# A hand-written schedule of an opening, ordered anew across five engines

## What is computed

```python
x = x + tanh(g_xattn) * matmul(fake_quant(layernorm(x)), fake_quant(ctx))      # 8-bit codes, round and clip 0..255
A, g = quant_act(layernorm(x))       # blocks of 16 to fp8; the last 128 columns twice
gate = A @ quant_w(w_gate).T * g     # weights: blocks of 16 to int4, 2752 x 1024
up   = A @ quant_w(w_up).T * g
h    = silu(gate) * up
x    = x + tanh(g_ffn) * (quant_act(h) @ quant_w(w_down).T) * gm
```

## Time and profile before

| | |
|---|---|
| three runs, median | 793.53 us (793.03 to 793.79) |
| the profiled execution | 792.68 us, span 790.6 us |
| PE busy | 729.5 us, 92% of the span |
| DVE busy | 537.0 us, 68% |
| POOL busy | 339.9 us, 43% |
| ACT busy | 304.2 us, 38% |

### The profile page before, as it was taken

The page is one execution under the profiler, slowest core; times in us unless marked ns, Lnnn a source line. Parts: engine busy times, 40 slices in busy tenths (PEclk is TensorE's granted clock), DMA queues, the critical chain, the costliest instruction groups (busy, mean ns, idle before and its releaser), DMA issues.

```text
span 790.6 us, 10396 instructions
## 1 busy us (share of the span) xinstructions
PE 729.5 (92%) x3472; PEld 333.5 (42%) x3472; DVE 537.0 (68%) x966; ACT 304.2 (38%) x394; POOL 339.9 (43%) x207
## 2 busy tenths in 40 slices
PE   3578249999999999999999999999999999999998
PEld 0233124554444444444444444444444444444443
DVE  2588888952757565665758575747988888988700
ACT  5699965441434334342524252422222312231300
POOL 4435997791857657474847574730000000000000
PEclk9998659999999999999999999999999999999999
DMA  7933696376697969798888889854456474545410
GB/s 291 408 126 109 184 199 133 90 157 155 133 231 161 208 163 223 173 200 204 183 195 182 211 192 213 181 132 160 94 144 208 122 192 115 149 130 124 107 45 27
DMA packets 228885, 131.56 MB, mean 166 GB/s; under 512 B 201713, under 2 KB 212977, under 8 KB 227825
## 3 DMA queue, kind: packets, MB, share of 16 engines
q1 hardware_dynamic: 228848, 131.12, 67.4%
HBM read 61.88 MB, written 19.66 MB: 103 GB/s over the span
## 4 chain that ended last, share of the span: by engine, by line
PE 86%; POOL 3%; DMA 3%; SPq 3%; ACT 2%; issue 2%; DVE 1%; ACTq 0%
PE acc L1373 55%; PE acc L1440 28%; DMA big<-in_ctx_dram 2%; PE acc L1315 2%; DMA mid<-big 1%; POOL h_in L765 1%; SPq L477 1%; SPq L359 1%; ACT big L928 1%; POOL big L742 0%; POOL wbuf_all L735 0%; POOL big L748 0%; POOL wbuf_all L728 0%; SPq L366 0%; ACT big L897 0%
## 5 line engine op out<-in xcount | busy, mean ns | idle before, releaser
L1373 PE MATMUL acc<-mid 128*128 128x512 f16 x1920 | 417.1, 380 | 2.0 <-DMA mid<-big 2.0
L1373 PEld LDWEIGHTS acc<-mid 128*128 128x128 f16 x1920 | 188.3, 98 | 229.4 <-issue 4.8
L1440 PE MATMUL acc<-big,mid 128*128 128x512 f16 x1040 | 224.6, 379 | 0.0
L1440 PEld LDWEIGHTS acc<-big,mid 128*128 128x128 f16 x1040 | 101.8, 98 | 122.7
L848 POOL TENSOR_TENSOR h_in<-wbuf_all,h_in 128x1024 f16<-128x1024 f32 (+1 forms) x56 | 114.4, 2044 | 85.8 <-ACT h_in L1194 85.7
L728 POOL TENSOR_TENSOR wbuf_all<-wbuf_all,w_inv 128x1024 f32<-128x1024 f32 (+1 forms) x67 | 124.7, 1867 | 54.9 <-DVE w_inv L1582 54.9
L1576 DVE TENSOR_REDUCE tb<-wbuf_all 128x64 f32<-128x1024 f32 (+1 forms) x67 | 78.9, 1178 | 45.8 <-DMA wbuf_all<-in_L_ffn_w_gate_dram 23.5
L965 ACT ACTIVATE wbuf_all<-wbuf_all 128x1024 f32<-128x1024 f32 (+1 forms) x67 | 68.1, 1016 | 86.9 <-POOL wbuf_all L728 86.9
L1685 DVE SCALAR_TENSOR_TENSOR h_out<-acc,silu 128x256 f32<-128x256 f32 (+1 forms) x88 | 36.4, 414 | 93.5 <-ACT silu L1027 58.1
L1194 ACT ACTIVATE h_in<-wbuf_all 128x1024 f16<-128x1024 f32 (+1 forms) x56 | 56.9, 1016 | 103.5 <-DVE wbuf_all L1588 103.5
L1588 DVE SCALAR_TENSOR_TENSOR wbuf_all<-wbuf_all,tb 128x1024 f32<-128x1024 f32 (+1 forms) x56 | 65.1, 1163 | 3.4 <-ACT wbuf_all L965 3.1
(11 more groups left out here) (155 smaller groups left out, 553.7 us busy)
## 6 DMA issues: line engine op xcount, KB each, us to landing
h_in<-h_d SPq DMA_DIRECT2D x8, 1376.0 KB, 7.0
wbuf_all<-in_L_ffn_w_gate_dram SPq DMA_DIRECT2D x21, 512.0 KB, 4.3
wbuf_all<-in_L_ffn_w_up_dram SPq DMA_DIRECT2D x21, 512.0 KB, 4.2
h_d<-h_out SPq DMA_DIRECT2D x80, 128.0 KB, 3.5
big<-in_ctx_dram SPq DMA_DIRECT2D x16, 512.0 KB, 7.1
wbuf_all<-in_L_ffn_w_down_dram SPq DMA_DIRECT2D x16, 512.0 KB, 4.5
big<-in_x_dram SPq DMA_DIRECT2D x8, 512.0 KB, 10.4
x_d<-big SPq DMA_DIRECT2D x8, 512.0 KB, 2.6
```

The source lines that it names most:

```text
L1373: last = pe.matmul(acc[m % 4][:, 0:cols], a_t[:, s, left, k, :], w[:, right, k, 0:cols], start=(k == 0 and left == 0 and right == 0), stop ...
L1440: last = pe.matmul(acc[2 * i + hf][:], left[:, k - ks.start, :], right[:, k, hf * MW:(hf + 1) * MW], start=(k == 0 and left is hi and righ ...
```

## The change

OPENING takes P2 before U2 and P3 before U4. POOL_BACK grows from four pieces to nine. STATS_ACT grows from two x tiles to six. The queues of all engines are written in another order, and some steps change engine: ten context tiles are coded by VectorE instead of two; codings of x tiles are distributed anew; start_a(1) and start_a(3) are on VectorE and were start_pool on GpSimd. SyncE loads x tile 0 ahead of the parameters. TensorE has 18 more transposes (WARM_FIRST), after the first two tiles of activations are quantised. No size and no operation inside a helper is changed.

```diff
+WARM_FIRST = 18
-OPENING = (("U", 0), ("P", 0), ("P", 1), ("U", 1), ("U", 2), ("P", 2), ("U", 3), ("U", 4),
-           ("P", 3), ("U", 5), ("P", 4), ("P", 5), ("P", 6), ("U", 6), ("U", 7), ("P", 7))
+OPENING = (("U", 0), ("P", 0), ("P", 1), ("U", 1), ("P", 2), ("U", 2), ("U", 3), ("P", 3),
+           ("U", 4), ("U", 5), ("P", 4), ("P", 5), ("P", 6), ("U", 6), ("U", 7), ("P", 7))
-POOL_BACK = (1, 3, 4, 7)
-STATS_ACT = (6, 7)
-STATS_DVE = (0, 1, 2, 3, 4, 5)
+POOL_BACK = (0, 1, 2, 3, 4, 5, 6, 7, 10)
+STATS_ACT = (0, 1, 3, 5, 6, 7)
+STATS_DVE = (2, 4)
...
             pe.wait_ge(x1_ready, NT)
+            pe.wait_ge(a_ready, 2)
+            for i in range(WARM_FIRST):
+                pe.transpose(acc[3][:, 0:P], ident[:], ident[:])
             pe.wait_ge(nat_a_lo, 1)
...
+            load_x(0)
             for i, p in enumerate((s1, z1, s2, z2, g_xattn, g_ffn)):
...
             load_ctx(4)
+            load_x(2)
             load_ctx(5)
-            load_x(0)
+            load_x(3)
+            load_x(1)
...
@@ SyncE, before turn_a(0)
+            turn_piece(3)
+            load_piece(7)
+            store_x1(6)
+            turn_piece(4)
+            load_piece(8)
             store_x1(7)
             order_columns(slice(6, 8))
-            turn_piece(3)
-            load_piece(7)
-            turn_piece(4)
-            load_piece(8)
             turn_a(0)
...
@@ ScalarE, first products
             silu_open(("P", 3))
             silu_open(("U", 4))
             magic_fold(3)
```

More of the change, by code:

```diff
@@ L789, in _ @@
             scale(1, buf(1))
+            back_open(0)
             scale(2, buf(2))
+            back_open(1)
             lo_open(0)
+            lo_open(1)
             start_pool(0)
-            back_open(1)
+            back_open(2)
             scale(3, buf(3))
-            lo_open(1)
-            start_pool(1)
+            lo_open(2)
             scale_a(0)
-            lo_open(2)
+            back_open(3)
             scale(4, buf(4))
-            back_open(3)
+            lo_open(3)
             scale_a(1)
+            scale(5, buf(5))
             small_a(0)
-            scale(5, buf(5))
-            lo_open(3)
             back_open(4)
             scale(6, buf(6))
+            back_open(5)
             lo_open(4)
@@ L823, in _ @@
             small_a(2)
+            scale(7, buf(7))
+            back_open(7)
+            lo_a(4)
             start_pool(6)
-            lo_a(4)
+            lo_a(5)
             start_pool(7)
-            lo_a(5)
             scale_a(6)
+            lo_open(7)
             scale_a(7)
             small_a(3)
-            scale(7, buf(7))
-            back_open(7)
+            scale(8, buf(8))
             lo_a(6)
             lo_a(7)
-            lo_open(7)
-            scale(8, buf(8))
             scale(9, buf(9))
+            lo_open(8)
             scale(10, buf(10))
-            lo_open(8)
+            scale(11, buf(11))
             lo_open(9)
+            back_open(10)
             lo_open(10)
-            scale(11, buf(11))
             def lo_nat(u, s):
@@ L1110, in _ @@
             whole_w(4)
-            hi_open(3)
+            root(2, 2)
             norm(2)
+            round_w(5, buf(5))
             root(2, 3)
+            whole_w(5)
+            magic_fold(0)
             keep_outliers(2)
-            square_x1(6)
-            round_w(5, buf(5))
-            magic_fold(0)
-            square_x1(7)
             hi_open(4)
@@ L1121, in _ @@
             hi_a(0)
+            whole_w(6)
+            hi_open(5)
             norm(3)
+            magic_a(2)
             keep_outliers(3)
-            hi_open(5)
-            magic_a(2)
-            hi_open(6)
             hi_a(1)
             root(2, 4)
+            root(2, 5)
+            square_x1(6)
+            square_x1(7)
+            hi_open(6)
             magic_a(3)
-            root(2, 5)
             norm(4)
+            norm(5)
             keep_outliers(4)
-            root(2, 6)
-            root(2, 7)
-            norm(5)
             keep_outliers(5)
@@ L1173, in _ @@
             round_w(10, buf(10))
+            whole_w(10)
             silu_open(("P", 6))
+            round_w(11, buf(11))
             hi_open(10)
@@ L1793, in _ @@
             layernorm(2, 3, 2.0 * A_UP)
-            back_w(5)
-            back_w(6)
+            make_x1(7)
+            spread_x1(4)
+            spread_x1(5)
             max_a(3)
@@ L1798, in _ @@
             end_a(2)
[L1799 to L1800 removed]
+            start_a(3)
             layernorm(2, 4, 2.0 * A_UP)
[L1802 to L1803 removed]
+            layernorm(2, 5, 2.0 * A_UP)
             end_a(3)
             max_a(4)
[L1806 removed]
             coef_a(4)
@@ L1848, in _ @@
             h_open(("P", 7))
-            front(PIECE_LOOP, 0, 16 * (loads_before(0, 0) + 1))
             def h_tile(u, s):
```

300 lines of the change are left out of this document (151 added, 149 removed).

## The result

The changed kernel took 799.91 us (median of 4 runs, 799.62 to 800.43), the kernel before 793.66 beside it on the same chip: ratio 1.008, 95% interval 1.0063 to 1.0098. The forecast was 788.2 with a range to 791.6. It is 11.7 us off and has the wrong sign. The profiled execution has a span of 798.2 us against 790.6.

What follows compares the result with a forecast made beforehand. The time was taken as the arrival of turned tile 1, set by GpSimd's low half of tile 0, plus 664.55 us of unbroken TensorE. Terms -6.0 + 0.7 = -5.3 gave 787.4, as median 788.2; range 785.8 to 791.6.

Steps and rivals of the forecast that it cites:

- (a): Loads: with x tile 0 issued first, ctx tile 6 lands about 0.9 us earlier, bounds 0 to 1.3.
- (b): Codings and statistics exchanged between ScalarE and VectorE: loads equal within about 1 us, last ctx tile shifted at 40.5.
- (c): ScalarE from attention of tile 0 to whole_w(1): 27 entries from 39.9, 23.1 us plus 0.9 of waits, ending at 63.95.
- (d): GpSimd, main term: start 52.2, busy 45.7, pauses 4.4, so low half of tile 0 ends at 102.3, 6.0 us earlier.
- rival 2: GpSimd pays for its added pieces: low half of tile 0 ends 3.9 us later, 797.4 in all; chance 0.07.
- The changed queue keeps this part as it is: SyncE and DMA from low half of tile 0 to tile 1's product: the same turns and loads, 17.8 us as before.
- (f): Starts of tiles 1 and 3 on VectorE: 1.2 us each, ends 0.8 and 1.9, nothing net.
- A rule weighed: GpSimd shifts beside VectorE codings: nothing added by the median; at the maximum two shifts cost 0.5 us each, 789.2.
- (e): Left out of the walk along the queues: slow attention of tile 5 on TensorE, 0.7 us allowed, bounds 0 to 1.7.
- Warming: 18 extra transposes on TensorE: can make the first product 5.3 us instead of 7.08, hidden behind tile 1's turn, worth 0.
- Rival 4: No change: SyncE's turn of piece 4, load and new store delay the turn of tile 0; 792 to 793.5, chance 0.06.
- (g): Behind tile 1, new order of products: worth 0, at worst 0.3 us late, tightest at tile 6.

Runs made afterwards that it cites:

- run 1: Changed kernel with the coefficients (second operand) of VectorE's starts of tiles 1 and 3 in PSUM instead of SBUF: 794.33 us, ratio 1.0016.
- run 3: Changed kernel with code_x(7) and quantise_x(6) moved from VectorE back to ScalarE: 797.84 us, ratio 1.0059.
- run 4: Changed kernel with tiles 1 and 3 coefficients in PSUM, square roots of tiles 6 and 7 early, code_x(7) and quantise_x(6) on ScalarE: 793.15 us, ratio 0.9992.
- run 10: Changed kernel with the starts of tiles 1 and 3 back on GpSimd, all else as changed: 797.97 us, ratio 1.006.
- run 11: Run 4's kernel with the scales of weight piece 3 moved earlier on VectorE: 793.00 us, ratio 1.0000.
- run 12: Run 11's kernel with the multiplications back of weight pieces 5 and 6 on VectorE again: 792.14 us, ratio 0.9984.
- runs 6 and 7: Kernel before with only the start of tile 3 moved to VectorE: both operands in SBUF 792.91 us, coefficients in PSUM 792.54 us.
- run 5: Separate kernel timing VectorE instruction forms alone and beside four GpSimd instructions; TENSOR_TENSOR with both inputs in SBUF: 1.22 us alone, 1.23 beside, GpSimd's four 8.68.
- run 8: Changed kernel without the 18 added transposes: 799.37 us, ratio 1.0067.

## Why the prediction was wrong, step by step

| kernel | low half of tile 0 ends | turn of tile 1 issued | tile 1's product | from there to the end |
|---|---|---|---|---|
| before | 108.26 | 118.97 | 126.05 | 664.6 |
| changed | 110.16 | 122.63 | 128.32 | 669.9 |
| forecast | 102.3 | not given | 120 to 121.5 | 664.6 |
| run 1, operand in PSUM | 110.13 | 122.83 | 128.44 | 664.6 |
| run 3, two codings | 109.53 | 121.52 | 128.85 | 667.1 |
| run 4, all three | 108.41 | 120.74 | 127.70 | 664.6 |
| run 10, starts on GpSimd | 111.00 | 124.15 | 131.29 | 664.6 |
| run 11 | 106.70 | 118.65 | 125.90 | 664.6 |
| run 12 | 106.24 | 118.84 | 125.89 | 664.6 |

Each row is one execution, and single executions of one kernel lie up to 3 or 4 us apart (run 4: 790.7 to 794.37), so differences of under 1 us between rows prove little.

**(a), (b) right.** The last ctx tile was shifted at 41.04 (45.13 before; forecast 40.5 to 41.5):

```profile
41.04 1.19 POOL L723 TENSOR_SCALAR mid<-big,nrz 128x1024 bf16<-128x1024 uint8 x1 [0.33 <-ACT big L886]
```

**(c) right in its sum, wrong in its start.** ScalarE's first entry behind attention 0 began at 42.41 instead of 39.9, and its queue to whole_w(1) took 24.3 us (forecast 24.05), so the multiplication back of piece 1 started at 66.80 instead of 63.95. The 2.5 are mostly attention 0: it started 1.2 late (35.0 in the walk) and took 5.08, where the walk had 4.2 and the kernel before 3.63 (33.04). The profile's clock reads 1.00 in both stretches, but rows of TensorE give a likely cause. The column sums took 0.52 each just ahead of it and 0.26 each behind it; before, four of them took 1.42 ahead of the attention, so the pace had begun to rise.

```profile
35.37 1.04 PE L1302 MATMUL tb<-mid,onesb 128*128 128x512 bf16 x2 [0.91 <-POOL mid L723]
36.20 5.08 PE L1317 MATMUL acc<-mid,big 128*128 128x512 bf16 x16
...
42.21 1.03 PE L1302 MATMUL tb<-mid,onesb 128*128 128x512 bf16 x4
```

That the attention began at half pace is my reading of these rows. In the other traces with this queue it took 4.70 to 5.96.

**(d) the first step that failed.** "start 52.2" was 55.16 (attention late, then the outlier columns, for which VectorE waited on ScalarE). "Busy 45.7" was 47.6. "Pauses 4.4" were 7.4. Sum of the three: 2.96 + 1.9 + 3.0 = 7.9, which is the whole way from 102.3 to 110.16. Against the kernel before: pauses 4.5 less, work 5.8 more (3.9 counted, 1.9 drawn out beside VectorE), start 0.65 later, so 1.9 later in all. That is rival 2 in its direction and its place, "GpSimd pays for its pieces", though its own number said otherwise: piece 1 was multiplied back at 66.80, ahead of the 70.0 that was to decide. From there the stretch was not unbroken: it held 3.95 of pauses and 1.37 of drawn-out instructions.

**"The changed queue keeps this part as it is" failed too.** I compared SyncE's list, which is the same behind turn_a(0), and neither what stands just ahead of it nor what its entries wait for. The turn of tile 1 was issued 12.47 behind the low half of tile 0 in place of 10.71. Most of it is the turn of tile 0, which kept SyncE 4.38 us in place of 2.32. In all ten traces in which a store of x1 is issued directly ahead of it (0.74 before, at 109.44), it took 4.2 to 4.5, in the three without 2.1 to 2.3 (before, runs 6 and 7). No run moves the store alone, so it is not shown that the store is the cause. The wait for the low half of piece 6, which stands one instruction later on GpSimd, is small here: SyncE stood idle ahead of that turn for 0.60 us (117.63 to 118.23), where it is 0.30 in the kernel before. With a third instruction it was 2.4 (run 10).

**(f) the step that costs most.** "I take 1.2 each, with 0.8 and 1.9 for the ends." Measured 2.36 and 9.16. The nearest row, L1676, was of the same size and had its second operand in PSUM; alone, both forms cost the same (run 5: 1.22 each). I took size and number of inputs for the form, and the place of the operand was the form. With the operand in PSUM the estimate of 1.2 holds (1.21, run 1).

**"A rule weighed" was weighed too lightly.** The longest shift of the earlier trace rows, 1663 against a median of 1117, was the mark of exclusion: it stood beside a quick coding of VectorE (29.67), and run 5 shows such shifts held by 0.43. I put it on the shifts alone and at 1.0 in all. The section of the Trainium skill that the prediction names there ("GPSIMD Engine Reference", "Key points") puts VectorE's instructions with two SBUF inputs beside the fast ones, and I had kept only the fast ones. Run 5 agrees (8.68 for GpSimd's 7.60). Of both kinds the change has more that can fall beside GpSimd: four codings and three quantisings of x, eight ctx codings, two starts.

**(e)** The allowance of 0.7 for attention 5 was of the right kind: 5.72 against 5.33 before, with 3.51 of idle time ahead of it. **Warming** worth 0: right (run 8), though not for the reason given: the first product did not become quick. It took 7.46 at a granted clock of 0.71, behind 4.51 of idle time; in run 12, where the idle time was 2.17, it took 5.34 at 1.00, and tile 1 still waited 1.65 for its turn, so nothing was gained by it. **Rival 4** named the right place, but not what happened there: SyncE issued the turn of tile 0 at 110.18, 0.02 behind the low half, so the new store made nothing late ahead of it. The lateness came in that issue itself, 2.06 longer. **(g)** "behind tile 1 nothing lost": wrong by 5.3, at tile 2 and not at tile 6, and by the start of (f), not by the order of products (run 1 has that order and no gap).

The chance of 0.85 for faster was the worst number of the text. The sum rested on seven us of GpSimd's pauses, and nearly all the ways in which the terms could miss made it smaller. Rival 2 had 0.07 and gave 797.4; that it came within 2.5 of the 799.91 is in part luck, since 5.3 of the loss is the start of (f), which it does not have.

## What to carry over

Before moving an elementwise instruction between VectorE and GpSimd, look up where each operand lies: with one in PSUM it ran beside GpSimd at its own price (1.21 to 1.22); with two in SBUF, or as a quick coding, one of the two engines waited for the other's instruction. When a queue is compared with another, compare what its entries wait for on the other engines and what stands just ahead of them, and not only their order. And where three engines are each busy for 80 to 95% of a stretch, work taken from one can come back as another's lateness, as in runs 11 and 12: the five edits of run 12 together brought back 7.8 us, and what is left as a gain over the kernel before is 1.3.
